# Second routed layer's front: fp32r subtraction on TensorE, two up parts moved there, gate weights ahead of the list's read-out

## The chip, the cores and the metric

The kernel runs on one core of one Trainium2 chip. The metric is the device time of one execution in microseconds (us), from the first to the last instruction of the core with what lies around it; lower is better.

## The reference, cut to what matters

Four layers act on 2048 rows of 256 floats, each added to its input: an attention, a mixture of 4 experts, an RWKV recurrence, and a mixture of 8 experts. The change lies at the start of the last one:

```python
x = hidden_states.reshape(-1, H)                       # 2048 rows of 256
logits = x @ gate_w.T + gate_b                         # 8 experts
top_vals, top_idx = jax.lax.top_k(logits, TOP_K)       # 2 of 8
routing = jax.nn.softmax(top_vals, axis=-1)
for e in range(E):
    h = x @ w1[e].T + b1[e]
    y = x_glu * jax.nn.sigmoid(1.702 * x_glu) * (x_lin + 1.0)
    out = out + (y @ w2[e].T + b2[e]) * we[:, None]
```

## The kernel before

A matrix product of float32 numbers is made from two fp32r parts of each factor: a high part (the number rounded to fp32r) and a low part (number minus high part, in fp32r). High by high, high by low and low by high are accumulated in PSUM. The weights of the experts therefore have to be split first. For the second mixture layer, `weight_units` cuts them into 12 parts of 128 x 1024: 8 up parts (w1 and w3, `k.up_parts`) and 4 down parts (w2). The original number lies in the low tile `f_w_lo`; ScalarE copies it into the high tile `f_w_hi` (`activation` Copy), and then it is replaced by the low part.

`second_front` does three things at once between the barrier after the RWKV phase and the first expert's product:

- **Ranking and lists.** VectorE (DVE) picks two experts for each token (`choose`, `pair`), counts (`place`), gives each choice a position (`positions`), and writes one-hot tables (`tables`: tile_oh, row_oh, tile_tok). TensorE (PE) multiplies tables (`Ranking.list`): 32 products of L941 give the token of every row of the tiles, and 16 products of L946 give the plane. VectorE then reads both out of PSUM (`rows`): `token_of`, and in three more operations `slot_of`. `weigh` makes the gate weights.
- **Splitting the up parts.** ScalarE `take_high`, then VectorE `take_low` (L879, a subtraction of two SBUF tiles), eight of each: two `take_low` before `rows`, six after, `weigh` at the end.
- **Splitting the down parts.** ScalarE `down_to_high` (L1322); TensorE `take_left` (for each half of 512 columns: identity times the number, L1302, then minus-identity times the high part, L1303, both as float32); ScalarE `down_to_low` (L1326) takes the difference out of PSUM. Two `take_left` stand ahead of `list` on TensorE, two behind it. `down_to_low` of one part must free the banks for a later `take_left`.

Each engine runs its instructions in the order written here; nothing is reordered but by hand. Part numbers n in `take_left(n)` and `down_to_low(n)` count from 0.

`expert_phase` follows in the same block with no barrier. GpSimd (POOL) waits for `rows_known` and then starts indirect gathers of token rows (L1423), one for each of the 39 tiles, 6 ahead. TensorE turns the rows of tiles 0 and 1 (L1469), ScalarE makes their high part (L1527), VectorE the low part (L1571), and `up(0)` (L1488) multiplies; it waits for all up parts. The first `turn_h` waits for all down parts. Then tiles follow in a fixed cycle, and the results are scattered with `slot_of` (L1437).

Of the kernel before, what the change touches and what calls it, by code (L numbers as in the profile page):

```python
# [884 lines left out]
class Ranking:  # L885

    def __init__(self, nc, m, v, k, ctx):
# [21 lines left out]
         self.zeros_ready, self.tiles_known, self.first_plane, self.numbered) = (  # L909
            sem(n) for n in "step exponentials_done picks ranked rows_ready counted named planed "  # L910
            "zeros_ready tiles_known first_plane numbered".split())
# [42 lines left out]
class RankSteps:  # L954
# [82 lines left out]
    def rows(self):  # L1037
        t, dve, then, k = self.t, self.dve, self.then, self.k
        dve.wait_ge(t.named, 1)
        then(dve.tensor_scalar(k.token_of[:], t.named_psum, float(TOK), None, ALU.add))  # L1040
        then(dve.scalar_tensor_tensor(out=t.unused[:], in0=t.named_psum, scalar=0.0, in1=t.neg_spare[:],
# [4 lines left out]
        then(dve.scalar_tensor_tensor(out=k.slot_of[:], in0=t.unused[:], scalar=2.0 * TOK, in1=t.named_psum,  # L1046
                                      op0=ALU.add, op1=ALU.add))
        k.rows_known = (t.step, self.done)
# [34 lines left out]
def first_front(nc, m, v, k, ctx, block):  # L1083
# [15 lines left out]
    parts, take_low = weight_units(v, k)  # L1099
    k.all_known = ((k.hi_done, k.all_parts), (k.lo_done, k.all_parts))  # L1100
# [109 lines left out]
    def _(dve):  # L1210
# [49 lines left out]
        steps.rows()  # L1260
# [7 lines left out]
def second_front(nc, m, v, k, ctx, block):  # L1268
# [8 lines left out]
    AT_ROWS, BEFORE_LIST = 2, 2  # L1277
    down_parts = parts[k.up_parts:]
    down_high, down_left, down_low, neg_zero, neg_ready = (
        sem(n) for n in "down_high down_left down_low neg_zero neg_ready".split())  # L1280
    k.all_known = ((down_high, len(down_parts)), (down_low, len(down_parts)))
    neg_ident = ctx.enter_context(nc.sbuf_tensor(f"{v.tag}r_neg_ident", [P, P], F32))
    flat = lambda part: f32(part).rearrange("p e n -> p (e n)")
    left = lambda n: (m.banks[:, 4:6, :] if n == 1 else m.banks[:, 6:8, :]).rearrange("p b n -> p (b n)")

    @block.gpsimd
    def _(pool):
        rank.clear(pool)
        pool.memset(neg_ident[:], 0.0).then_inc(neg_zero, 1)
        pool.wait_ge(neg_zero, 1)  # L1290
        pool.affine_select(out=neg_ident[:], in_=neg_ident[:], compare_op=ALU.not_equal, fill=-1.0, base=0,
                           pattern=[[-1, P]], channel_multiplier=1).then_inc(neg_ready, 1)

    @block.tensor
    def _(pe):
        def take_left(n):
            hi, lo = down_parts[n]
            pe.wait_ge(down_high, n + 1)
            at_least(pe, down_low, (0, 0, 1, 3)[n])
# [15 lines left out]
    def _(act):  # L1315
# [23 lines left out]
        for n in range(1, 5):  # L1339
            take_high(n)  # L1340
# [1041 lines left out]
```

## Time and profile before

| | |
|---|---|
| median of 3 runs | 732.92 us (732.75 to 733.7) |
| the profiled execution's own time | 731.65 us |
| its span, first to last instruction | 729.7 us |
| mean granted TensorE clock | 0.952 of full speed |
| busy share: PE, DVE, ACT, POOL | 90%, 71%, 48%, 46% |
| front of the second mixture layer, first DVE operation to first expert product | 566.33 to 597.18 us |
| its experts, first product to last scatter landed | 597.18 to 707.8 us |

The times of the table's last two rows are positions in the span. The profiled execution lies 1.95 us over its span, and 1.27 us under the median.

### The profile page before, as it was taken

The page shows a single profiled execution, that of the slowest core. Times are in us where ns is not written, and L with a number is a line of the kernel's source. Part 1 is how long each engine was busy: PE and PEld are TensorE (multiplying, and loading weights), DVE is VectorE, ACT ScalarE, POOL GpSimd, SP SyncE. Part 2 cuts the span into 40 slices and gives each one's busy share as a digit, 9 for nine tenths or more (in the row PEclk, how much of TensorE's full clock was granted, in tenths as well). Part 3 has the DMA queues.
Part 4 walks back from the last instruction along what each step waited for, and adds up shares of the span by engine and source line. Part 5 has one row for each costly group of instructions (what it writes and reads, how often), then busy time and mean ns, then how long its engine had stood idle before and what let it go on. Part 6 is the DMA issues. An engine that isn't in the chain of part 4 may idle for free. (4 is left out here: it accounts for less than half of the span.)

```text
span 729.7 us, 13761 instructions
## 1 busy us (share of the span) xinstructions
PE 660.3 (90%) x4339; PEld 538.6 (74%) x4339; DVE 518.9 (71%) x1087; ACT 349.0 (48%) x735; POOL 337.1 (46%) x326
## 2 busy tenths in 40 slices
PE   8989999879989999999997999999988679999950
PEld 6656666568868888888886888888877348888840
DVE  5878888957865555544444699998782868888847
ACT  1767777736403333333333565554552844554420
POOL 4977767510053344334224255555331066777530
PEclk9999999998999999999999999999976799999985
DMA  6900000101013111111106940000010022333229
GB/s 197 337 2 3 1 2 15 45 11 53 1 56 105 58 59 51 52 58 55 34 22 206 363 146 2 1 0 1 30 58 30 1 65 76 101 101 102 78 81 311
DMA packets 37185, 54.23 MB, mean 74 GB/s; under 512 B 6644, under 2 KB 28918, under 8 KB 36982
## 3 DMA queue, kind: packets, MB, share of 16 engines
q1 hardware_dynamic: 27832, 31.78, 13.0%
q0 software_dynamic: 7104, 19.41, 8.5%
q10 hardware_dynamic: 2176, 2.10, 0.9%
q8 instruction: 42, 0.69, 0.4%
q14 instruction: 31, 0.25, 0.1%
HBM read 37.28 MB, written 15.99 MB: 73 GB/s over the span
## 5 line engine op out<-in xcount | busy, mean ns | idle before, releaser
L1926 PE MATMUL banks<-r_xt,r_w_mixed 128*128 128x256 f32 x384 | 84.9, 380 | 0.7 <-ACT r_xt L2023 0.7
L1577 DVE SCALAR_TENSOR_TENSOR f0x_s<-f0x_th,banks 128x512 f32<-128x512 f32 x35 | 24.1, 687 | 83.2 <-ACT f0x_th L1536 83.2
L1437 POOL DMA_INDIRECT f_y<-f0x_yout,f_slot_of x35 | 34.5, 984 | 99.6 <-ACT f0x_yout L1552 99.6
L1926 PEld LDWEIGHTS banks<-r_xt,r_w_mixed 128*128 128x128 f32 x384 | 72.1, 189 | 11.0 <-ACT r_xt L2023 1.0
L1536 ACT ACTIVATE f0x_th<-banks 128x512 f32<-128x512 f32 x35 | 21.0, 600 | 86.9 <-PE banks L1488 86.9
L1423 POOL DMA_INDIRECT f0x_xg<-f_xn,f_token_of x35 | 34.9, 996 | 55.7 <-DVE f_slot_of L1046 44.3
L659 DVE TENSOR_REDUCE a_ssum<-a_e 128x6 f32<-128x1536 f32 x32 | 56.0, 1748 | 1.3 <-ACT a_e L526 1.0
L1488 PE MATMUL banks<-f_w_hi,f0x_xt_hi 128*128 x140 | 55.4, 396 | 0.9 <-DVE f0x_xt_lo L1571 0.9
L1488 PE MATMUL banks<-f_w_lo,f0x_xt_hi 128*128 x140 | 55.6, 397 | 0.0
L1423 POOL DMA_INDIRECT f1x_xg<-f_xn,f_token_of x39 | 40.6, 1041 | 32.4 <-DVE f_slot_of L1046 19.3
L1488 PE MATMUL banks<-f_w_hi,f0x_xt_lo 128*128 x140 | 55.2, 394 | 0.0
L526 ACT ACTIVATE a_e<-banks 128x1536 f32<-128x1536 f32 x32 | 46.6, 1455 | 13.9 <-PE banks L402 13.9
L1437 POOL DMA_INDIRECT f_y<-f1x_yout,f_slot_of x39 | 38.9, 997 | 27.4 <-ACT f1x_yout L1552 27.1
L757 POOL TENSOR_TENSOR a_rr<-a_ms_eps,neg_half 128x32 f32<-128x32 f32 (+1 forms) x9 | 44.0, 4888 | 15.3 <-DVE a_ms_eps L627 15.3
L1512 PE MATMUL banks<-f_w_hi,f0x_ht_hi 128*128 x140 | 42.4, 302 | 0.7 <-ACT f0x_yout L1552 0.7
L1512 PE MATMUL banks<-f_w_lo,f0x_ht_hi 128*128 x140 | 39.4, 281 | 0.0
L1512 PE MATMUL banks<-f_w_hi,f0x_ht_lo 128*128 x140 | 39.3, 281 | 0.0
L402 PE MATMUL banks<-a_ut,a_qt 32*128 32x256 f32 x512 | 36.7, 400 | 2.9 <-ACT a_e L516 2.1
L427 PE MATMUL banks<-a_e,a_vv 128*32 128x256 f32 x512 | 34.3, 385 | 1.7 <-DVE a_vv L674 1.5
L402 PEld LDWEIGHTS banks<-a_ut,a_qt 32*128 32x128 f32 x512 | 23.2, 184 | 16.9 <-ACT a_e L516 8.0
L1545 ACT ACTIVATE f1x_ht_hi<-banks 128x256 fp32r<-128x256 f32 x39 | 15.0, 385 | 40.5 <-PE banks L1499 40.5
L1589 DVE TENSOR_TENSOR f1x_hb<-banks,f_b 128x512 f32<-128x512 f32 x39 | 27.0, 691 | 9.3 <-PE banks L1488 9.3
(368 smaller groups left out, 1895.9 us busy)
## 6 DMA issues: line engine op xcount, KB each, us to landing
f_w_lo<-in_f_w13T SPq DMA_DIRECT2D x4, 2048.0 KB, 11.1
r_y<-f_y SPq DMA_DIRECT2D x16, 256.0 KB, 4.9
f_w_lo<-in_f_w2T SPq DMA_DIRECT2D x4, 512.0 KB, 15.1
f_xn<-f_rows_normed SPq DMA_DIRECT2D x8, 256.0 KB, 2.1
f_b<-in_f_b SPq DMA_DIRECT2D x1, 2048.0 KB, 10.1
f_w_lo<-in_f_w2T SPq DMA_DIRECT2D x2, 1024.0 KB, 11.9
f_xn<-r_y SPq DMA_DIRECT2D x8, 256.0 KB
f1c_y<-f_y SPq DMA_DIRECT2D x8, 256.0 KB, 7.8
```

The costliest lines, as they stand in the source:

```text
L402: last = pe.matmul(scores[:, i, s, :], qt[rows, b % 2, e, k, s * P:(s + 1) * P], ut[rows, b % 2, k, :], start=True, stop=True)
L427: last = pe.matmul(av(n)[32 * i:32 * i + 32, :], values[:, b % 2, head, :, :].rearrange("p r d -> p (r d)"), side[:, S * i + s, :], start= ...
L526: act.activation(ebuf[:, n % 3, 0:SUMS_ON_DVE, :], scores[:, 0:SUMS_ON_DVE // S].rearrange("p i s t -> p (i s) t"), ACT.Exp).then_inc(exp_ ...
L659: dve.tensor_reduce(ssum[:, b % 2, NB * p:NB * p + SUMS_ON_DVE], ebuf[:, n % 3, 0:SUMS_ON_DVE, :], AX_X, ALU.add).then_inc(sum_done, 1)
L757: pool.tensor_tensor(part(rr[:]), part(ms_eps[:]), part(m.neg_half[:, 0:S * NH]), ALU.pow).then_inc(rr_found, 1)
L1423: pool.indirect_dma_start(xg[:, t % GB, :], None, k.xn_dram, bass.IndirectOffsetOnAxis(ap=k.token_of[:, t:t + 1], axis=0)).then_inc(gather ...
L1437: pool.indirect_dma_start(k.y_dram, bass.IndirectOffsetOnAxis(ap=k.slot_of[:, done:done + 1], axis=0), yout[:, done % YB, :], None).then_i ...
L1488: last = pe.matmul(out, xt[a][:, t % 2, kb * P:(kb + 1) * P], k.weights[c][0][kb][:, e, cols], start=(i == 0), stop=(i == len(steps) - 1))
L1512: last = pe.matmul(y_psum(t), ht[a][:, t % 2, hb * P:(hb + 1) * P], k.weights[c][1][hb][:, e, :], start=(i == 0 and not v.lin_bias), stop= ...
L1577: dve.scalar_tensor_tensor(out=s1[:, t % 2, :], in0=th[:, t % 2, :], scalar=1.0, in1=glu_part, op0=ALU.add, op1=ALU.mult).then_inc(s1_done, 1)
L1589: dve.tensor_tensor(hb1[:, t % 2, :], up_banks(t), k.b1[:, e, :].rearrange("p e n -> p (e n)"), ALU.add).then_inc(hb1_done, 1)
L1926: last = pe.matmul(bank(1 + kind)[:, eb * T:(eb + 1) * T], r.w_mixed[:, kind, j // KB, j % KB, eb * P:(eb + 1) * P], xt[:, b % 2, j % KB, ...
```

## The change

Seven edits, the first six in `second_front` or in functions it calls. The subtracting product of `take_left` takes the high part and minus-identity as fp32r instead of float32. The last two up parts go the way of the down parts (`left_parts`, six of them; `PLAIN` is 6), so VectorE's `take_low` is called six times instead of eight. TensorE does four `take_left` ahead of `list` and two behind it, and waits for the fifth low part before it goes on. The PSUM banks for them alternate between two pairs. ScalarE's order is written anew. `weigh` moves from the end of VectorE's queue to just before the list's read-out, which is split into `tokens` (1 operation) and `slots` (3 operations); one `take_low` stands between them where two stood before both. GpSimd's gathers wait for the tokens and the tables' last reading by TensorE instead of for `slot_of`; only the first scatter waits for `slot_of` (in the first mixture layer the gathers wait for all three).

```diff
-    def rows(self):
+    def tokens(self):
         dve.wait_ge(t.named, 1)
         then(dve.tensor_scalar(k.token_of[:], t.named_psum, float(TOK), None, ALU.add))
+        k.tokens_known = (t.step, self.done)
+
+    def slots(self):
         then(dve.scalar_tensor_tensor(out=t.unused[:], in0=t.named_psum, scalar=0.0, in1=t.neg_spare[:],
                                       op0=ALU.is_equal, op1=ALU.mult))
         dve.wait_ge(t.planed, 1)
...
-        k.rows_known = (t.step, self.done)
+        dve.scalar_tensor_tensor(out=k.slot_of[:], ...).then_inc(t.slotted, 1)
@@ second_front
-    AT_ROWS, BEFORE_LIST = 2, 2
+    BY_PRODUCT = 2
+    down_parts, side_parts = parts[k.up_parts:], parts[k.up_parts - BY_PRODUCT:k.up_parts]
+    PLAIN = k.up_parts - BY_PRODUCT
+    left_parts = down_parts + side_parts
+    k.up_known = ((k.hi_done, PLAIN), (k.lo_done, PLAIN), (left_low, len(left_parts)))
+    k.all_known = ((left_high, len(left_parts)), (left_low, len(left_parts)))
+    neg_ident = ctx.enter_context(nc.sbuf_tensor(f"{v.tag}r_neg_ident", [P, P], F32R))
+    left = lambda n: m.banks[:, 4 + 2 * (n % 2):6 + 2 * (n % 2), :].rearrange("p b n -> p (b n)")
@@ TensorE
-            at_least(pe, down_low, (0, 0, 1, 3)[n])
+            at_least(pe, left_low, n - 1)
             for half in range(2):
-                pe.matmul(left(n)[:, cols], m.ident[:], flat(lo)[:, cols], start=True, stop=False)
+                pe.matmul(left(n)[:, cols], m.ident[:], f32(flat(lo))[:, cols], start=True, stop=False)
                 last = pe.matmul(left(n)[:, cols], neg_ident[:], flat(hi)[:, cols], start=False, stop=True)
-        for n in range(BEFORE_LIST):
+        for n in range(len(down_parts)):
             take_left(n)
         rank.list(pe)
-        for n in range(BEFORE_LIST, len(down_parts)):
+        for n in range(len(down_parts), len(left_parts)):
             take_left(n)
+        pe.wait_ge(left_low, len(left_parts) - 1)
@@ ScalarE, after the exponentials
-        down_to_high(2)
-        down_to_low(0)
-        down_to_high(3)
-        take_high(0)
-        down_to_low(1)
+        left_to_high(2)
+        left_to_high(3)
+        left_to_low(0)
+        left_to_high(4)
+        left_to_low(1)
         rank.negate(act)
-        for n in range(1, 5):
-            take_high(n)
-        down_to_low(2)
-        for n in range(5, k.up_parts):
-            take_high(n)
-        down_to_low(3)
+        left_to_low(2)
+        left_to_high(5)
+        left_to_low(3)
+        for n in range(PLAIN):
+            take_high(n)
+        left_to_low(4)
+        left_to_low(5)
@@ VectorE
         steps.experts()
-        for n in range(AT_ROWS):
-            take_low(dve, n)
-        steps.rows()
-        for n in range(AT_ROWS, k.up_parts):
-            take_low(dve, n)
-        steps.weigh()
+        steps.weigh()
+        steps.tokens()
+        take_low(dve, 0)
+        steps.slots()
+        for n in range(1, PLAIN):
+            take_low(dve, n)
@@ expert_phase, GpSimd
-        pool.wait_ge(*k.rows_known)
+        pool.wait_ge(*k.tokens_known)
+        pool.wait_ge(*k.tables_read)
+        if r:
+            pool.wait_ge(*k.slots_known)
...
+                if done == 0 and not r:
+                    pool.wait_ge(*k.slots_known)
@@ expert_phase, TensorE, before up(0)
-                    pe.wait_ge(k.hi_done, k.up_parts)
-                    pe.wait_ge(k.lo_done, k.up_parts)
+                    for semaphore, value in k.up_known:
+                        pe.wait_ge(semaphore, value)
```

`tables_read` is the semaphore `planed`, which the last L946 product raises.

## Rows read from the trace of the kernel before

**Rows 1.** The page: busy time of TensorE and the others, whole span.

```profile
PE 660.3 (90%) x4339; PEld 538.6 (74%) x4339; DVE 518.9 (71%) x1087; ACT 349.0 (48%) x735; POOL 337.1 (46%) x326
```

**Rows 2.** The chain that ended last, 570 to 600 us: start, length, what.

```profile
581.44 2.79 PE banks L941 x32
...
585.54 1.85 PE banks L1302 x2
...
590.23 1.03 ACT f_w_lo L1326
...
595.11 1.02 ACT f_w_lo L1326
...
597.18 1.67 PE banks L1488 x6
```

**Rows 3.** Windows: stretch, length, busy time by engine, granted clock, DMA share, GB/s.

```profile
570.88:574.07 3.19, 3.19 (x7) 2.03 (x8) 1.99 (x8) 3.19 (x4) 0.00 (x0) 0.50 0.00 0
574.07:580.01 5.94, 5.94 (x14) 2.28 (x12) 5.50 (x17) 3.31 (x4) 0.00 (x0) 1.00 0.00 0
...
581.44:585.54 4.10, 4.10 (x49) 4.10 (x50) 3.93 (x9) 4.10 (x5) 0.00 (x0) 0.85 0.02 4
585.54:590.23 4.69, 4.66 (x8) 1.71 (x8) 3.97 (x6) 0.00 (x1) 3.56 (x2) 0.77 0.10 28
```

**Rows 4.** Timeline of TensorE, `take_left`: start, length, line, names.

```profile
571.89 1.92 PE L1302 MATMUL banks<-f_w_lo,ident 128*128 128x512 f32 x2
...
573.60 1.26 PE L1303 MATMUL banks<-f_w_hi,f1r_neg_ident 128*128 128x512 f32 x2
...
593.19 1.02 PE L1302 MATMUL banks<-f_w_lo,ident 128*128 128x512 f32 x2
594.05 1.02 PE L1303 MATMUL banks<-f_w_hi,f1r_neg_ident 128*128 128x512 f32 x2
```

**Rows 5.** Timeline of VectorE: last table, experts, subtractions, weights; idle before in brackets.

```profile
580.59 0.80 DVE L1025 TENSOR_TENSOR f1k_tile_tok<-f1k_tile_oh,f1k_token 128x1248 f16<-128x1248 f16 x1
...
582.70 0.18 DVE L1034 CAST f_expert_of<-f1k_ef 128x39 int32<-128x39 f32 x1
582.92 2.36 DVE L879 TENSOR_TENSOR f_w_lo<-f_w_lo,f_w_hi 128x1024 fp32r<-128x1024 f32 x2
...
586.12 3.50 DVE L879 TENSOR_TENSOR f_w_lo<-f_w_lo,f_w_hi 128x1024 fp32r<-128x1024 f32 x3
592.23 3.50 DVE L879 TENSOR_TENSOR f_w_lo<-f_w_lo,f_w_hi 128x1024 fp32r<-128x1024 f32 x3 [2.62 <-ACT f_w_hi L1318]
595.65 0.17 DVE L1056 TENSOR_SCALAR f1k_total<-f1k_ex 128x16 f32<-128x16 f32 x1
```

**Rows 6.** Timeline of ScalarE: third high part, first low part, four up parts.

```profile
573.42 1.04 ACT L1322 ACTIVATE f_w_hi<-f_w_lo 128x1024 fp32r<-128x1024 f32 x1
576.62 1.02 ACT L1326 ACTIVATE f_w_lo<-banks 128x1024 fp32r<-128x1024 f32 x1 [2.15 <-PE banks L1303]
...
581.59 3.96 ACT L1318 ACTIVATE f_w_hi<-f_w_lo 128x1024 fp32r<-128x1024 f32 x4
```

**Rows 7.** Timeline of GpSimd: gathers 0, 1 and 3.

```profile
586.37 1.91 POOL L1423 DMA_INDIRECT f1x_xg<-f_xn,f_token_of  x1 [19.27 <-DVE f_slot_of L1046]
588.59 1.85 POOL L1423 DMA_INDIRECT f1x_xg<-f_xn,f_token_of  x1 [0.30 <-issue]
...
592.00 0.95 POOL L1423 DMA_INDIRECT f1x_xg<-f_xn,f_token_of  x1 [0.31 <-issue]
```

**Rows 8.** The tile of gathered rows, first mixture layer: from issue to landing.

```profile
DMA to landing us min/median/max: 2.7/2.8/4.7
```

**Rows 9.** The chain, in the experts' steady cycle: six fp32r products of 512 columns.

```profile
605.28 1.40 PE banks L1488 x6
```

**Rows 10.** Windows in the first mixture layer: pause before its list, list, stretch behind it.

```profile
200.21:202.38 2.17, 0.01 (x1) 0.00 (x1) 2.17 (x3) 0.60 (x1) 0.00 (x0) 1.00 0.00 0
...
206.19:209.40 3.21, 3.18 (x8) 2.23 (x8) 2.75 (x4) 0.00 (x0) 2.08 (x2) 0.59 0.00 0
```

More of the change, by code:

```diff
@@ L1040, in rows @@
         then(dve.tensor_scalar(k.token_of[:], t.named_psum, float(TOK), None, ALU.add))
+        k.tokens_known = (t.step, self.done)
+    def slots(self):
+        t, dve, then, k = self.t, self.dve, self.then, self.k
         then(dve.scalar_tensor_tensor(out=t.unused[:], in0=t.named_psum, scalar=0.0, in1=t.neg_spare[:],
@@ L1045, in rows @@
                                       op0=ALU.mult, op1=ALU.subtract))
-        then(dve.scalar_tensor_tensor(out=k.slot_of[:], in0=t.unused[:], scalar=2.0 * TOK, in1=t.named_psum,
-                                      op0=ALU.add, op1=ALU.add))
-        k.rows_known = (t.step, self.done)
+        dve.scalar_tensor_tensor(out=k.slot_of[:], in0=t.unused[:], scalar=2.0 * TOK, in1=t.named_psum,
+                                 op0=ALU.add, op1=ALU.add).then_inc(t.slotted, 1)
     def weigh(self):
@@ L1099, in first_front @@
     parts, take_low = weight_units(v, k)
+    k.up_known = ((k.hi_done, k.up_parts), (k.lo_done, k.up_parts))
     k.all_known = ((k.hi_done, k.all_parts), (k.lo_done, k.all_parts))
@@ L1276, in second_front @@
     parts, take_low = weight_units(v, k)
-    AT_ROWS, BEFORE_LIST = 2, 2
[L1278 to L1284, printed above, removed]
+    BY_PRODUCT = 2
+    down_parts, side_parts = parts[k.up_parts:], parts[k.up_parts - BY_PRODUCT:k.up_parts]
+    PLAIN = k.up_parts - BY_PRODUCT
+    left_parts = down_parts + side_parts
+    left_high, left_made, left_low, neg_zero, neg_ready = (
+        sem(n) for n in "left_high left_made left_low neg_zero neg_ready".split())
+    k.up_known = ((k.hi_done, PLAIN), (k.lo_done, PLAIN), (left_low, len(left_parts)))
+    k.all_known = ((left_high, len(left_parts)), (left_low, len(left_parts)))
+    neg_ident = ctx.enter_context(nc.sbuf_tensor(f"{v.tag}r_neg_ident", [P, P], F32R))
+    flat = lambda part: part.rearrange("p e n -> p (e n)")
+    left = lambda n: m.banks[:, 4 + 2 * (n % 2):6 + 2 * (n % 2), :].rearrange("p b n -> p (b n)")
     @block.gpsimd
@@ L1358, in _ @@
         steps.experts()
-        for n in range(AT_ROWS):
+        steps.weigh()
+        steps.tokens()
+        take_low(dve, 0)
+        steps.slots()
+        for n in range(1, PLAIN):
             take_low(dve, n)
-        steps.rows()
-        for n in range(AT_ROWS, k.up_parts):
-            take_low(dve, n)
-        steps.weigh()
 def expert_phase(nc, m, v, k, ctx, block, A, r):
```

31 lines of the change are left out of this document (16 added, 15 removed).

## The prediction, made before the changed kernel was run

> **What bounds the kernel now.** I read the page first. TensorE is busy 90% of the span [rows 1], so what it waits for is what can be won. Next the chain that ended last, around the place of the change. Up to the tables the front of the second mixture layer is a chain of small VectorE operations, which the change leaves alone; it ends when L1025 ends at 581.39 [rows 5]. From there the chain runs on TensorE: list and planes 581.44 to 585.54, then the two `take_left` behind the list, with the low parts that ScalarE takes at 590.23 and 595.11, and then the first expert product at 597.18 [rows 2]. What the reader is to see: from 585.54 to 595.11 the experts wait for TensorE to subtract two down parts. VectorE's own subtractions end at 592.23 + 3.50 = 595.73 [rows 5], so they are late by nearly as much; a change that relieved only one of the two would gain little. Then the windows, for the clock: it stood at 0.50 (1.2 GHz) until 574.07, at 1.00 (2.4 GHz) until the list, and was 0.85 and 0.77 in the mean in the list and the stretch behind it [rows 3]. Last the timelines of the four other engines, for who is next.
>
> Behind 597.18 the experts run in TensorE's cycle, and everything after hangs on it. I take a shift of the first product to reach the end one for one.
>
> **The subtracting pass.** At full clock L1302 starts at 593.19 and L1303 at 594.05: a float32 product of 512 columns costs 0.86 us, and a `take_left` has four, 3.44 us [rows 4]. At half clock it is 573.60 - 571.89 = 1.71 [rows 4]. An fp32r product of 512 columns costs 1.40/6 = 0.23 [rows 9]. The new pass has that shape and type, with another stationary tile, so I take 0.23 (0.43 to 0.46 at half clock). From above its cost is bounded by today's 0.86; from below I exclude under 0.21, since 1.40/6 is already nearly 512 columns at 2.4 GHz. A `take_left` becomes 2 x (0.86 + 0.23) = 2.18.
>
> **TensorE ahead of the list, four `take_left` instead of two.** The first: starts at 571.89, L1302 at half clock to 573.60, the pass 0.45 to 574.05; the clock rises at 574.07 as before, since up to 573.60 TensorE does the same; 0.86 + 0.23 end it at 575.14. Three more at 2.18 end at 581.68. Do they wait? `take_left(2)` needs the low part 0, `take_left(3)` the low part 1. ScalarE takes high parts 2 and 3 from 573.42, each about 1.0 [rows 6], until 575.4, low 0 until 576.5, high 4 until 577.5, then low 1 (TensorE's second is done at 577.5 with the drain) until 578.6. TensorE wants them at 577.3 and 579.5. So no wait, with 0.9 to spare. The list begins at 581.68 instead of 581.44: **+0.24**. List and planes take 4.10 [rows 3] and end at 585.78.
>
> **Behind the list, again two `take_left`.** Before: from 585.54 to ScalarE's start at 595.11, 9.57 us, in which TensorE also waited about 1.2 for ScalarE's low part of 590.23 [rows 2]. That wait goes: the banks of part 4 were emptied with low 2 (about 581), those of part 5 with low 3 (about 583). After, with the clock down as long as now: L1302 about 1.85 [rows 2], pass 0.43, then 0.86 and 0.23, second part 2.18, drain 0.15: 5.70 us, to 591.48. **-3.87.** From ScalarE's start on the last low part to the first product it took 597.18 - 595.11 = 2.07 [rows 2], and the same steps stand there: low part, high part of x, low part of x. The first product starts at 593.55.
>
> **Does ScalarE get there?** Its low 2 is at 580.8, high 5 at 581.8, low 3 (TensorE's fourth ends at 581.85) at 582.9. Six `take_high` at 3.96/4 = 0.98 [rows 6] end at 588.9, low 4 at 589.9. It waits for TensorE at 591.5, so it is not the bound. It has two low parts more than before, 2 x 1.02 [rows 6], where it used to wait.
>
> **VectorE.** `experts` ends at 582.88. `weigh` costs 0.66 (595.65 to about 596.31, three operations that begin with the row shown) [rows 5], to 583.6; it lies in the time in which the list is still being made. If that cover were gone it would cost its 0.66, which it costs today behind the last subtraction. The token list is ready at about 584.6 (list's end 584.23 [rows 2] plus 0.24 and a hand-over of 0.1) and read in 0.2. A subtraction costs 3.50 for three, 1.14 from start to start and 1.22 the last [rows 5]. One goes to 585.95, `slots` is 0.7 (of the 0.92 that the four reading operations have between 585.20 and 586.12, and planes are there by 585.9), to 586.65, and five more to 586.65 + 4 x 1.14 + 1.22 = 592.43. Their high parts are there at 588.9. So two subtractions less (-2.3), no wait for ScalarE (2.62 before [rows 5]), and about 1.6 later since only one comes before the slots and none before the tokens. VectorE alone would let the first product start at 592.43 + 0.05 + 0.43 for x's low part + 0.19 = 593.1. It is the next in line, 0.45 behind TensorE.
>
> **GpSimd.** Gathers now need the tokens (584.8) and the planes' last product (585.78), so the first starts at about 586.1 instead of 586.37. Gathers 0 and 1 took 1.91 and 1.85, gather 3 took 0.95 though a subtraction began during it [rows 7]. Gather 0 began inside a subtraction of 586.12 and ended 0.94 after that one's end: a gather that starts during L879 is held till it ends, one already running is not. In the new order gather 0 falls into `slots` (587.1), gather 1 starts at 587.4 in the subtraction that ends at 587.87, is out at 588.8, and lands 2.7 less 0.95 later [rows 8], at 590.6. `turn_x(0)` comes at 591.3. Hidden, by 0.7. The first scatter's wait for `slot_of` (586.65) costs nothing; a scatter needs the first result, 8 us after the first product.
>
> **First mixture layer.** GpSimd waits for two more semaphores, VectorE for one less; bounds -0.1 and +0.2 (two hand-overs), taken as 0.
>
> **Sum.** +0.24 - 3.87 = -3.63, first product at 593.55. The profiled execution took 731.65, so 728.0. The median of the three runs is 1.27 above it: 732.92 - 3.6 = **729.3 us**. Of a gain under 0.2% (1.5 us) I would not say that a measurement tells it from none.
>
> **The rivals.**
>
> *The clock doesn't fall (729.3 becomes 728.8), chance 0.15.* Before the list TensorE paused from 580.01 to 581.44, then the clock fell in the middle of the list. The new order has no pause there. Also in the first mixture layer a pause of 2.17 stands before the list, and the stretch behind it has 0.59 [rows 10]. Then the two last `take_left` cost 4.36 + 0.15, end at 590.3, and VectorE binds: 593.1, or -4.1. Against it: the list's products themselves are small, TensorE is busy in all 4.10 us of them [rows 3], and the fall comes there. The Trainium skill (TensorE: Matmul & The Clock Gate, What's actually happening) has the clock lowered after idleness; by it alone this rival would be the likelier. The fall in a busy list is why I don't follow it.
>
> *The clock falls later or longer, chance 0.13.* If it falls at the list's end and stays down the 3.4 us that it does now (584.3 to 587.7), it is at half until 589.2: low part 5 starts at 592.0 and the first product at 594.1, -3.1, 729.8. If it stays down through both `take_left`, they cost 2 x 2 x (1.71 + 0.43) = 8.6, the first product comes at 596.6, -0.6, 732.3. I give the latter 0.04.
>
> *Gathers bind, 0.07.* If GpSimd loses every turn against the back-to-back subtractions and its second gather only gets out after 592.4, it lands at 595.1 and the first product comes at about 596.5: -0.7, 732.2. Against it gather 1, which got out during three subtractions in a row.
>
> *Slower: the pass isn't cheap, 0.05.* If it costs what L1303 costs now, 0.86, the four parts end at 576.41 + 3 x 3.44 = 586.7, the list is 5.3 late and VectorE stands behind it in its wait for the tokens. TensorE's last two parts end at 586.7 + 4.1 + 8.3 = 599.1, the first product comes at 601.1: +3.9, 736.8. Twelve passes lie on the path, so it decides from 0.23 + 3.63/12 = 0.53 a pass on, and is slower by 0.2% from 0.66. Nothing in the rows shows this price for fp32r.
>
> *The change does little at the end, 0.05.* The front is shorter, but the experts' cycle starts with new waits (gathers, two fewer buffers ahead) and takes 2 us back. The steady cycle shows TensorE full, so I see no place for it.
>
> **Numbers.** Forecast 0.55 with its own range 728.8 to 729.9, the full clock 0.15, later or longer clock 0.13 (0.04 of it at 732.3), gathers 0.07, slower 0.05, little 0.05. Range 728.4 to 731.2: from the full clock less 0.4 for two runs of one kernel differing, to half of what the gathers and the long slow clock could cost. Faster: 0.55 + 0.15 + 0.09 + a part of the gathers and of the little, 0.86. Same: 0.09. Slower: 0.05.
>
> **What the new profile would show.** L1303 with 8 records near 0.4 us long, one for each product, 0.23 from start to start with its neighbour. The list at 581.7. ScalarE's low 1 before 579.5. No idle of VectorE in front of a subtraction. The granted clock in the stretch behind the list: 0.77 as before, or 1.00 (rival). The first L1488 at 593.5, with the wait before it by x's low part, and the last low part of ScalarE at 591.5. The prediction is wrong if TensorE idles between the four first `take_left`, if the list starts after 582.5, or if L1469 waits for a gather.

## The result and the profile after

The changed kernel takes 728.53 us (median of 6 runs, 727.83 to 729.23), the kernel before 732.84 in the same comparison: ratio 0.9942, 95% interval 0.993 to 0.9955, that is 4.3 us less (3.3 to 5.1). Forecast were 729.3 us and a gain of 3.6. A later comparison gave 0.9956 (0.9941 to 0.9971), that is 3.2 us by the ratio and 2.5 us by the medians. One of the six executions of an experiment below (gathers wait for slot_of) took 855.42 us with a mean granted clock of 0.734; its row and ratio leave it out. The profiled execution took 727.92 us with a span of 726.2; its TensorE clock was 0.952 in the mean, as before.

Line numbers have moved: L1302 and L1303 are L1311 and L1312, L1326 is L1336, L1423 is L1434, L941 is L942, L1469 is L1485, L1488 is L1504, L1571 is L1587; the experiments shift them by a few lines more. Positions are also shifted: the front's first VectorE operation starts at 565.91 here and at 566.33 in the profile of before, though nothing ahead of it but the first layer's read-out was changed. I therefore measure the front by two lengths that begin there:

- **L**, to the first expert product: 597.18 - 566.33 = 30.85 before, 593.92 - 565.91 = 28.01 after.
- **M**, to the start of the last scatter: 705.34 - 566.33 = 139.01 before, 702.11 - 565.91 = 136.20 after. It holds the experts too, and so a clock that is down at their start.

The timeline of the changed kernel, for these lengths and for what each engine did last:

```profile
565.91 0.29 DVE L1359 TENSOR_TENSOR f_logits<-banks,f_gate_b 128x128 f32<-128x128 f32 x1 [7.43 <-PEq L2312]
...
580.17 0.80 DVE L1026 TENSOR_TENSOR f1k_tile_tok<-f1k_tile_oh,f1k_token 128x1248 f16<-128x1248 f16 x1
...
581.93 2.78 PE L942 MATMUL banks<-f1k_tile_tok,f1k_row_oh 128*128 128x39 f16 x32
...
585.06 1.23 DVE L879 TENSOR_TENSOR f_w_lo<-f_w_lo,f_w_hi 128x1024 fp32r<-128x1024 f32 x1
...
586.77 5.76 DVE L879 TENSOR_TENSOR f_w_lo<-f_w_lo,f_w_hi 128x1024 fp32r<-128x1024 f32 x5
586.83 2.10 POOL L1434 DMA_INDIRECT f1x_xg<-f_xn,f_token_of  x1 [20.15 <-DVE f1k_unused L1049]
...
589.24 1.85 POOL L1434 DMA_INDIRECT f1x_xg<-f_xn,f_token_of  x1 [0.30 <-issue]
...
591.84 1.02 ACT L1336 ACTIVATE f_w_lo<-banks 128x1024 fp32r<-128x1024 f32 x1 [1.15 <-PE banks L1312]
...
592.95 0.44 PE L1485 MATMUL banks<-ident,f1x_xg 128*128 128x128 f32 x2 [0.93 <-DMA f1x_xg<-f_xn,f_token_of]
593.17 0.42 DVE L1587 TENSOR_TENSOR f1x_xt_lo<-banks,f1x_xt_hi 128x256 fp32r<-128x256 f32 x1 [0.64 <-ACT f1x_xt_hi L1543]
...
593.92 0.49 PE L1504 MATMUL banks<-f_w_hi,f1x_xt_hi 128*128 x1 [0.53 <-ACT f1x_xt_hi L1543]
...
702.11 0.97 POOL L1453 DMA_INDIRECT f_y<-f1x_yout,f_slot_of  x1 [0.34 <-ACT f1x_yout L1568]
```

Three things end within a microsecond: ScalarE's last low part at 592.86, VectorE's last subtraction at 586.77 + 5.76 = 592.53, the second gather's landing at 592.91. Before, ScalarE's was at 596.13, VectorE's at 595.73, and GpSimd had started the second gather's transfer by 590.44, 6.7 us before the first product [rows 2, 5, 7].

The chain that ended last, same kernel:

```profile
573.40 0.43 PE banks L1312
573.83 1.50 PE banks L1311 x2
575.33 0.23 PE banks L1312
...
581.86 0.23 PE banks L1312
582.09 2.64 PE banks L942 x32
...
586.83 2.10 POOL f1x_xg L1434
...
589.24 3.67 DMA f1x_xg<-f_xn,f_token_of
...
592.95 0.45 PE banks L1485 x2
...
593.92 1.67 PE banks L1504 x6
```

The reader is to see three things. The pass costs 0.23 at full clock and 0.43 at half. The list follows straight on the fourth part, where before it waited for the tables; TensorE, not the tables, now starts it. And behind the list the chain no longer runs through TensorE's products but through a gather; that is a close race, not a long wait.

The granted clock, by windows of the same kernel:

```profile
571.49:574.95 3.46, 3.46 (x7) 1.68 (x6) 2.85 (x11) 3.46 (x5) 0.00 (x0) 0.50 0.00 0
575.05:581.80 6.75, 6.75 (x20) 3.41 (x18) 6.47 (x15) 5.46 (x6) 0.00 (x0) 1.00 0.00 0
582.00:585.20 3.20, 3.20 (x42) 3.20 (x42) 1.33 (x8) 3.07 (x4) 0.00 (x0) 1.00 0.02 5
585.30:588.60 3.30, 3.30 (x13) 2.01 (x12) 3.23 (x6) 3.30 (x4) 1.77 (x1) 0.50 0.00 0
588.60:592.00 3.40, 3.40 (x11) 1.61 (x9) 3.40 (x4) 1.47 (x3) 2.79 (x3) 0.99 0.18 51
```

The clock rose at 575.0, 9.1 us after the front's start; before it was 574.07 - 566.33 = 7.7 [rows 3]. It fell at 585.2, 3.3 us into the list, and rose at 588.6; in the kernel before it fell at 584.3, 2.9 us into the list, and rose at 587.7. So it is down for 3.4 us in both.

### The profile page after: what moved, and what is told of

The parts are those of the page before. It is cut to its first block and busy times, and to the rows that moved or that the text cites. A ratio compares the mean times of both kernels' runs of the same rounds, so it can differ in the third digit from the quotient of the medians.

```text
span 726.2 us, 13774 instructions
## 1 busy us (share of the span) xinstructions
PE 658.5 (91%) x4343; PEld 537.6 (74%) x4343; DVE 516.5 (71%) x1085; ACT 351.2 (48%) x737; POOL 336.4 (46%) x326
## 5 line engine op out<-in xcount | busy, mean ns | idle before, releaser
L1434 POOL DMA_INDIRECT f0x_xg<-f_xn,f_token_of x35 | 34.1, 973 | 56.3 <-DVE f_slot_of L1051 44.8
L1504 PE MATMUL banks<-f_w_hi,f0x_xt_hi 128*128 x140 | 55.4, 396 | 0.9 <-DVE f0x_xt_lo L1587 0.9
L1504 PE MATMUL banks<-f_w_lo,f0x_xt_hi 128*128 x140 | 55.6, 397 | 0.0
L1434 POOL DMA_INDIRECT f1x_xg<-f_xn,f_token_of x39 | 40.7, 1043 | 31.7 <-DVE f1k_unused L1049 20.2
L1504 PE MATMUL banks<-f_w_hi,f0x_xt_lo 128*128 x140 | 55.2, 394 | 0.0
L526 ACT ACTIVATE a_e<-banks 128x1536 f32<-128x1536 f32 x32 | 46.6, 1456 | 15.1 <-PE banks L402 15.1
```

The source lines that it names most:

```text
L526: act.activation(ebuf[:, n % 3, 0:SUMS_ON_DVE, :], scores[:, 0:SUMS_ON_DVE // S].rearrange("p i s t -> p (i s) t"), ACT.Exp).then_inc(exp_ ...
L1434: pool.indirect_dma_start(xg[:, t % GB, :], None, k.xn_dram, bass.IndirectOffsetOnAxis(ap=k.token_of[:, t:t + 1], axis=0)).then_inc(gather ...
L1504: last = pe.matmul(out, xt[a][:, t % 2, kb * P:(kb + 1) * P], k.weights[c][0][kb][:, e, cols], start=(i == 0), stop=(i == len(steps) - 1))
```

## The experiments

Times are against the kernel before in the same set of runs. The set of the changed kernel is the one above. Three sets followed, with medians of the kernel before of 732.31, 732.73 and 732.22 us: first the pass in float32, the pass alone, no up part, and gathers that wait for slot_of; then the filled pause, weights last, early products and combined; then the split read-out, the changed kernel again, the early products again, and the weights behind slot_of. L and M come from one profiled execution of each. A ratio can differ a little from that of the medians.

| run | time, us | ratio to before (95%) | L | M |
|---|---|---|---|---|
| before (profile shown ahead) | 732.84 | | 30.85 | 139.01 |
| changed | 728.53 | 0.9942 (0.993 to 0.9955) | 28.01 | 136.20 |
| changed, again | 729.68 | 0.9956 (0.9941 to 0.9971) | 27.68 | 136.19 |
| pass in float32 | 735.29 | 1.004 (1.0027 to 1.0053) | 34.05 | 142.16 |
| before, fp32r pass alone | 732.50 | 1.0005 (0.9991 to 1.0018) | 30.87 | 139.04 |
| the same, pause filled | 732.11 | 0.9996 (0.9982 to 1.001) | 30.10 | 139.85 |
| before, split read-out alone | 732.28 | 1.0006 (0.9994 to 1.0018) | 31.41 | 139.83 |
| changed, no up part on TensorE | 730.75 | 0.9984 (0.9971 to 0.9996) | 29.42 | 138.87 |
| changed, gathers wait for slot_of | 728.31 | 0.9948 (0.9933 to 0.9963) | 27.87 | 135.95 |
| changed, weights last | 728.93 | 0.9951 (0.9933 to 0.9969) | 28.14 | 136.26 |
| changed, early products | 726.98 | 0.9925 (0.9907 to 0.9943) | 27.32 | 135.67 |
| the same again | 727.69 | 0.9946 (0.9932 to 0.9961) | 27.27 | 135.49 |
| combined | 728.50 | 0.9938 (0.9919 to 0.9957) | 27.55 | 135.79 |
| combined, weights behind slot_of | 727.14 | 0.9933 (0.992 to 0.9947) | 26.56 | 134.80 |

**The pass in float32 again.** Everything else as changed.

```diff
-    neg_ident = ctx.enter_context(nc.sbuf_tensor(f"{v.tag}r_neg_ident", [P, P], F32R))
+    neg_ident = ctx.enter_context(nc.sbuf_tensor(f"{v.tag}r_neg_ident", [P, P], F32))
...
-                last = pe.matmul(left(n)[:, cols], neg_ident[:], flat(hi)[:, cols], start=False, stop=True)
+                last = pe.matmul(left(n)[:, cols], neg_ident[:], f32(flat(hi))[:, cols], start=False, stop=True)
```

> The changed kernel with one part undone: minus-identity and the high part go into the subtracting product as float32 again. I measure the front by L, from VectorE's first operation in it (the logits) to the first expert product; L was 30.85 us before and 28.01 after the change. Theory (the order of TensorE's work only pays since the pass is cheap): the four parts ahead of the list take 4.5 + 3 x 3.44 = 14.8 us, the list starts 5.3 later than before, the two parts behind it cost 8.3: L about 34.9, the kernel about 4 us slower than before, near 737. Rival (VectorE's two subtractions less are the gain, the pass does not matter): L at most 29.5, the kernel still faster than before.

Measured: L 34.05, 3.0 us slower. The list's first row in its timeline, and the read-out behind it:

```profile
588.26 2.81 PE L942 MATMUL banks<-f1k_tile_tok,f1k_row_oh 128*128 128x39 f16 x32
...
591.18 0.20 DVE L1041 TENSOR_SCALAR f_token_of<-banks 128x39 uint32<-128x39 f32 x1 [6.70 <-PE banks L942]
```

With the front's start at 567.24 the list starts 21.0 us into it, 5.9 later than before (581.44 - 566.33 = 15.1), and VectorE stands 6.70 us in its wait. The rival falls: the new order pays only with the cheap pass, and without it the change makes the kernel slower. L is 0.8 under what I expected, since the clock never fell: it was 1.00 from 576.2 on, through the list and both parts behind it.

**The fp32r pass alone, in the kernel before**, with its orders and eight subtractions.

```diff
-    neg_ident = ctx.enter_context(nc.sbuf_tensor(f"{v.tag}r_neg_ident", [P, P], F32))
-    flat = lambda part: f32(part).rearrange("p e n -> p (e n)")
+    neg_ident = ctx.enter_context(nc.sbuf_tensor(f"{v.tag}r_neg_ident", [P, P], F32R))
+    flat = lambda part: part.rearrange("p e n -> p (e n)")
...
-                pe.matmul(left(n)[:, cols], m.ident[:], flat(lo)[:, cols], start=True, stop=False)
+                pe.matmul(left(n)[:, cols], m.ident[:], f32(flat(lo))[:, cols], start=True, stop=False)
```

> The kernel before with one part alone: the subtracting product in fp32r. All orders and the eight VectorE subtractions stay. Theory (two engines are late side by side): TensorE's part behind the list ends at 589.1 instead of 590.2, ScalarE's three last high parts follow it, VectorE ends its subtractions and the weights at about 595.2, and the first product comes at 595.9: L about 29.6, gain 1.3 us, near 731.5. Rival (the pass is the whole gain): L near 28.0, the time of the changed kernel, 728.5.

Measured: L 30.87, no gain. Both theories fall. Its windows:

```profile
574.90:578.50 3.60, 3.56 (x10) 1.56 (x9) 3.19 (x15) 2.76 (x4) 0.00 (x0) 0.99 0.00 0
578.50:582.46 3.96, 0.00 (x0) 0.00 (x1) 3.93 (x6) 3.96 (x5) 0.00 (x0) 0.92 0.00 0
582.46:586.60 4.14, 4.14 (x49) 4.14 (x50) 3.97 (x9) 2.13 (x3) 0.00 (x0) 0.50 0.01 4
586.60:590.90 4.30, 4.30 (x6) 1.59 (x6) 3.92 (x6) 0.00 (x0) 3.20 (x2) 0.50 0.10 30
590.90:595.20 4.30, 3.10 (x5) 1.51 (x5) 2.17 (x2) 3.86 (x4) 3.39 (x4) 0.50 0.32 91
```

The two parts ahead of the list end sooner, TensorE pauses 4.0 us instead of 1.43, the clock falls at 581.8, before the list has begun, and stays at 0.50 until 595.5, though TensorE was busy in all 8.44 us from 582.46 to 590.90. What the pass saves, the slower float32 products beside it cost. I formed a third theory, that the gain was lost to the clock, and tried it.

**The pause filled.**

```diff
         for n in range(BEFORE_LIST):
             take_left(n)
+        for n in range(16):
+            pe.matmul(m.banks[:, 2, 0:P], m.ident[:], m.ones[:], start=True, stop=True)
         rank.list(pe)
```

> The kernel before with the fp32r pass alone, and 16 products of the identity with the tile of ones (128 columns, float32, into a bank that the list overwrites) put into TensorE's pause between the second part and the list; they add nothing to the output. With the pass alone TensorE paused 4.0 us there, its clock stood at 0.50 from 581.9 to 595.3, and L (VectorE's first operation of the front to the first expert product) was 30.87, as before the change. Theory (the cheaper pass's time was lost to the clock): the clock falls later or for about 3.4 us only, as in the kernel before, L is 29.6 within 0.4, the kernel 1.0 to 1.5 us faster than the pass alone. Rival (VectorE and ScalarE eat the gain, the clock is incidental): L stays at 30.9.

Measured: L 30.10, 0.77 shorter than with the pass alone, the theory's direction but about 0.6 of its size; the clock was down from 585.7 to 589.1 only, as long as in the kernel before. What limits L is now VectorE:

```profile
591.87 3.50 DVE L879 TENSOR_TENSOR f_w_lo<-f_w_lo,f_w_hi 128x1024 fp32r<-128x1024 f32 x3 [1.87 <-ACT f_w_hi L1320]
...
593.63 1.01 ACT L1328 ACTIVATE f_w_lo<-banks 128x1024 fp32r<-128x1024 f32 x1
```

ScalarE's last low part starts 26.9 us into the front, against 28.8 in the kernel before. VectorE's last of eight subtractions ends at 28.7, against 29.4. TensorE's side came 1.9 us earlier, and the first product only 0.75. M is 139.85, longer than before: TensorE, done early, waited 2.92 us for the low part of x, the clock fell again at 596.0 and was down until 602.8, in the first experts. The time is that of the kernel before (0.9996). So the clock took the pass's gain in the run with the pass alone, and in this one VectorE took a part of it and the clock in the first experts the rest. The windows and rows show where the time lies; that filling brings the gain back is not shown.

**No up part on TensorE.** VectorE subtracts eight.

```diff
-    BY_PRODUCT = 2
+    BY_PRODUCT = 0
@@ ScalarE
-        left_to_high(4)
...
-        left_to_high(5)
...
-        left_to_low(4)
-        left_to_low(5)
```

> The changed kernel with one part undone: no up part goes through TensorE, VectorE subtracts all eight; the four down parts stay ahead of the list. Theory (VectorE is the next in line): its subtractions end 2 x 1.14 = 2.3 us later than the 592.5 of the changed kernel, the first product comes at about 595.5: L about 29.6, 1.5 us slower than the changed kernel, near 730.1. Rival (TensorE's parts behind the list or the gathers bind, the subtractions are hidden): L near 28.0 or under it, 728.5.

Measured: L 29.42, 1.41 longer than the changed kernel's 28.01: the theory, to 0.2. M is 138.87, 2.67 longer, and here is the reason:

```profile
586.20:595.57 9.37, 1.39 (x6) 0.59 (x5) 9.30 (x13) 5.53 (x8) 7.61 (x4) 0.50 0.14 42
595.57:599.00 3.43, 3.43 (x9) 2.74 (x10) 0.48 (x2) 0.00 (x0) 2.52 (x4) 0.50 0.25 76
```

TensorE, with nothing behind the list, is busy 1.39 of 9.37 us; the clock, down since 585.4, stays at 0.50 until 599.0, and the first experts run at half speed. So the two up parts do two things: they take 2 x 1.14 us from VectorE, and they keep TensorE at work until the experts begin. The first is worth about 1.4 us of L, and what comes on top in M, 1.3 us, is the clock. In time it is 730.75 against 728.31 for the kernel whose gathers wait for slot_of, of the same set, 2.4 us. That the clock is what comes on top is read from these windows; no run keeps the clock up there without the two parts.

**Gathers wait for slot_of alone.**

```diff
-        pool.wait_ge(*k.tokens_known)
-        pool.wait_ge(*k.tables_read)
-        if r:
-            pool.wait_ge(*k.slots_known)
+        pool.wait_ge(*k.slots_known)
...
-                if done == 0 and not r:
-                    pool.wait_ge(*k.slots_known)
```

> The changed kernel with one part undone: in both mixture layers the gathers wait for slot_of alone, one wait instead of two or three. In the changed kernel's trace the first gather of the second mixture layer began at 586.83, 0.8 us after the last planes product, and that of the first one 0.98 us after slot_of, where it was 0.30 in the kernel before. Theory (the gathers are held by VectorE's subtractions, not by the semaphores): the first gather of the second layer still ends about 0.94 after the same subtraction, L stays at 28.0 within 0.2, the time is that of the changed kernel. Rival (the split read-out lets the gathers begin earlier and that is worth something): L grows by 0.5 or more. A third point is whether the separate waits themselves cost GpSimd time: then the first layer's gather comes back to 0.3 after slot_of.

Measured: L 27.87, the time of the changed kernel. The theory holds. In this run's timeline:

```profile
206.85 0.19 DVE L1051 SCALAR_TENSOR_TENSOR f_slot_of<-f0k_unused,banks 128x35 uint32<-128x35 f32 x1
...
207.34 1.93 POOL L1434 DMA_INDIRECT f0x_xg<-f_xn,f_token_of  x1 [44.41 <-DVE f_slot_of L1051]
...
586.79 1.79 POOL L1434 DMA_INDIRECT f1x_xg<-f_xn,f_token_of  x1 [20.43 <-DVE f_slot_of L1051]
```

Letting the gathers go before slot_of gains next to nothing: the first one of the second layer starts 586.79 - 565.58 = 21.2 us into the front here, 20.9 in the changed kernel. The third point came out too: the first layer's gather is back to 0.30 after slot_of, from 0.98.

**The weights last.**

```diff
-        steps.weigh()
         steps.tokens()
         take_low(dve, 0)
         steps.slots()
         for n in range(1, PLAIN):
             take_low(dve, n)
+        steps.weigh()
```

> The changed kernel with one part undone: the gate weights are made behind the last subtraction again. Theory (their 0.66 us lie in VectorE's wait for the list, and VectorE has slack to the last low part): the first low part of x would start at 593.2 instead of 593.17, L stays within 0.2 of 28.0. Rival (the move is a part of the gain): L grows by 0.5 to 0.7, the time by as much.

Measured: L 28.14, M 136.26. The rival falls: L is 0.13 longer, which is less than two profiles of the changed kernel differ by (0.33), so that move is worth nothing that shows here.

**The split read-out alone, in the kernel before.** The edits of `tokens`, `slots` and `expert_phase`'s GpSimd from the diff ahead, both layers:

```diff
-        steps.rows()
+        steps.tokens()
+        steps.slots()
...
-        pool.wait_ge(*k.rows_known)
+        pool.wait_ge(*k.tokens_known)
+        pool.wait_ge(*k.tables_read)
+        if r:
+            pool.wait_ge(*k.slots_known)
```

> The kernel before with one part alone, in both mixture layers: the read-out split into tokens and slots, and the gathers waiting for tokens and the tables' last reading (in the first layer for slot_of too). Subtractions, TensorE and ScalarE are those of before. I measure the stretch M from VectorE's first operation of the second front to the start of the last scatter, which takes in a clock that is down in the first experts: 139.0 us before, 136.2 after the change. Theory (all of the gain lies in the second front's products and subtractions): L and M as before, 30.9 and 139.0 within 0.2, no difference in time. Rival (part of the measured 4.3 us, of which the profiled front showed only 2.8, comes from the split read-out in the first layer): about 1 us faster than before with L and M unchanged. The first gather of each layer should again start 0.8 to 1.0 after its last semaphore, where one wait has 0.3.

Measured: no difference in time (1.0006), so no gain of a size that these intervals show comes from the first layer. But the theory misses L and M: L is 31.41 and M 139.83, not 30.85 and 139.01. The clock rose 9.0 us after the front's start here, not 7.7, and it fell at 19.3, not 18.0. TensorE does the same in both kernels until then. The later rise costs nothing ahead of the list, since the list waits for the tables and starts 15.11 us into the front in both. The later fall costs: more of the 3.4 us at half clock lies on float32 products of 512 columns. The chain of this run:

```profile
585.12 1.65 PE banks L1307 x2
586.77 1.71 PE banks L1308 x2
...
595.20 1.02 ACT f_w_lo L1331
```

L1308 is L1303 of before, where these two products took 1.09 (587.39 to 588.48). The last low part starts 29.33 us into the front, 0.55 later than before, which is all of L's 0.56. So the profile of the kernel before caught a short front, and with the clock's rise and fall at the same place (9.0 and 19.3; 9.1 and 19.3) the change is worth 31.41 - 28.01 = 3.40 in L and 3.63 in M.

**The changed kernel again.**

> The changed kernel once more, beside the others of this call. If its front is steady L is 28.0 and M 136.2 within 0.2. The time from the kernel's start to the second front's first operation differed by up to 2.6 us among the profiles so far, both ways; theory: that is what one execution differs from another, and the changed kernel is near 4 us faster than before with 2.8 to 3.6 of it in M. Rival: M is another by more than 0.5, so one profile does not tell the front's gain.

Measured: L 27.68, M 136.19, 3.2 us faster than before by the ratio, 2.5 by the medians. M repeats to 0.01, L to 0.33: here the clock rose at 8.1, and it fell once more for 3.4 us at the start of the experts, which gives it back. The theory holds for M, with L 0.1 outside of its bound. The start of the front lay at 567.99, 2.1 us from the first profile: that is what executions differ by.

**Early products.**

```diff
+        for n in range(10):
+            pe.matmul(m.banks[:, 2, 0:P], m.ident[:], m.ones[:], start=True, stop=True)
         rank.count(pe)
         pe.wait_ge(neg_ready, 1)
```

> The changed kernel with 10 products of the identity with the tile of ones (128 columns, float32, into a bank that the list overwrites) on TensorE at the front's start, before the counting products; they add nothing to the output. In the changed kernel the clock rose at 575.0, 9.1 us after the front's start, where I had forecast 574.07 - 566.33 = 7.7, and TensorE, not the tables, started the list: 0.9 late. Theory (the forecast's missing 0.8 us of the front are the clock's later rise): the clock is up when the first part begins or soon after, the four parts end before the tables are ready, the list starts as soon as they are, L is 27.1 within 0.3, about 0.9 us faster than the changed kernel, near 727.6. Rival (gathers or VectorE bind the first product anyway): L stays at 28.0.

Measured: L 27.32, M 135.67, 726.98 us. Windows of this run, and two rows of its timeline:

```profile
565.00:570.50 5.50, 5.50 (x24) 5.24 (x25) 4.39 (x15) 5.49 (x5) 0.61 (x3) 0.50 0.00 0
570.60:580.10 9.50, 9.12 (x26) 4.28 (x25) 8.71 (x25) 9.17 (x12) 0.00 (x0) 1.00 0.01 2
```

```profile
570.57 1.02 PE L1311 MATMUL banks<-f_w_lo,ident 128*128 128x512 f32 x2
...
580.07 2.86 PE L942 MATMUL banks<-f1k_tile_tok,f1k_row_oh 128*128 128x39 f16 x32 [0.35 <-DVE f1k_tile_tok L1026]
```

The clock is up when the first part begins, the row of its two records is 1.02 us long there instead of 1.92, and the list waits for the tables again. It starts 580.07 - 565.00 = 15.07 us into the front, 0.95 sooner than in the changed kernel, and L gets 0.69 of that. That is near the 0.79 by which the forecast missed L.

> The changed kernel with the 10 early products once more, beside the changed kernel itself. L was 27.3 and M 135.7, against 28.0 and 136.2. Theory: the front is 0.5 to 0.7 us shorter by the clock's earlier rise, and the time by as much; the 1.5 us between the medians of two calls were chance for the rest. Rival: the gain in time is the whole 1.5 us.

Measured: L 27.27, M 135.49, 727.69 us, beside 729.68 for the changed kernel. The front's gain repeats (0.4 to 0.7 in L and M). The medians differ by 2.0 us here, the ratios of the same two kernels by 0.7 us (0.9946 and 0.9956), and the intervals overlap. The 1.5 us of the first time compares medians of two sets. So I give the gain as 0.4 to 0.7 us by the front; that the time gains more is not shown.

**Combined.** The early products, and:

```diff
@@ TensorE: halves of the fifth part on either side of the list
+        take_left(4, (0,))
         rank.list(pe)
-        for n in range(len(down_parts), len(left_parts)):
-            take_left(n)
+        take_left(4, (1,))
+        take_left(5)
@@ ScalarE: the first up part's copy earlier
-        left_to_high(5)
+        take_high(0)
         left_to_low(3)
-        for n in range(PLAIN):
+        left_to_high(5)
+        for n in range(1, PLAIN):
@@ VectorE
         steps.weigh()
+        take_low(dve, 0)
         steps.tokens()
-        take_low(dve, 0)
+        take_low(dve, 1)
         steps.slots()
-        for n in range(1, PLAIN):
+        for n in range(2, PLAIN):
```

> A version that may beat the changed kernel: the 10 early products; half of the fifth part ahead of the list, in the time the faster clock frees; the first up part's high copy moved forward on ScalarE, so that VectorE subtracts one part while it waits for the list and one more between the read-outs. Theory (three engines are late within half a microsecond of one another, so all three must be relieved): TensorE's last part ends at about 24.3 us after the front's start (25.8 in the changed kernel), VectorE's subtractions at 25.3 (26.6), the gathers are out earlier by as much as the list, L is 26.6 within 0.4, 1.4 us faster than the changed kernel. Rival (the early products alone do it): L as in the run with them alone.

Measured: L 27.55, a miss, no better than the early products alone. Three engines were earlier (ScalarE's last low part began 24.6 us into the front, against 25.9), and the gathers were not:

```profile
588.09 4.62 DVE L879 TENSOR_TENSOR f_w_lo<-f_w_lo,f_w_hi 128x1024 fp32r<-128x1024 f32 x4
...
588.22 2.03 POOL L1441 DMA_INDIRECT f1x_xg<-f_xn,f_token_of  x1 [19.81 <-DVE f1k_unused L1049]
...
594.22 0.44 PE L1492 MATMUL banks<-ident,f1x_xg 128*128 128x128 f32 x2 [1.66 <-DMA f1x_xg<-f_xn,f_token_of]
```

The first gather began 0.13 us after a subtraction. The last low part starts 24.62 us into the front, 0.7 earlier than with the early products alone, and the first product comes 2.93 us behind it instead of 1.96: TensorE waits 1.66 us for the second gather.

**The weights behind slot_of.** 0.66 us of small operations now stand where the subtraction did.

```diff
-        steps.weigh()
         take_low(dve, 0)
         steps.tokens()
         take_low(dve, 1)
         steps.slots()
+        steps.weigh()
```

> The combined version with the gate weights' three small operations moved behind slot_of. In the combined version TensorE, ScalarE and VectorE were all earlier, but the first gather began 0.13 us after a subtraction, was held to its end, took 2.03 us, the second was held again, landed at 594.2 and was what the first product waited for (L 27.55). Theory (a gather that starts in a subtraction is held to its end): now it starts beside the small operations, takes 0.95, the second one is out 1.1 us earlier; the first product waits for the low parts; L is 26.8 within 0.3, M 135.0. Rival (the gathers are slow for another reason, their waits or the DMA): L stays at 27.5 or grows by 0.66, the weights' time.

Measured: L 26.56, M 134.80, 727.14 us.

```profile
587.10 1.06 POOL L1441 DMA_INDIRECT f1x_xg<-f_xn,f_token_of  x1 [19.81 <-DVE f1k_unused L1049]
...
587.67 4.63 DVE L879 TENSOR_TENSOR f_w_lo<-f_w_lo,f_w_hi 128x1024 fp32r<-128x1024 f32 x4
588.47 1.25 POOL L1441 DMA_INDIRECT f1x_xg<-f_xn,f_token_of  x1 [0.30 <-issue]
...
593.08 0.49 PE L1511 MATMUL banks<-f_w_hi,f1x_xt_hi 128*128 x1 [1.08 <-DVE f1x_xt_lo L1594]
```

The first gather takes 1.06 instead of 2.03 and the first product waits for the low part of x again. L is 1.0 shorter than without the move, though VectorE's last subtraction ends 0.7 later (25.8 against 25.1 us into the front). The last low part starts at the same place (24.60 against 24.62), so the gathers are the whole 1.0: the first product comes 1.96 behind it again. The theory holds, and this is the shortest front: 1.4 us under the changed kernel in M. In time it is 2.5 us less in the medians of one set and 1.7 by the ratios, with intervals (0.992 to 0.9947, and 0.9941 to 0.9971) that overlap a little.

## Why the prediction was right, step by step

Steps in us from the front's start; those forecast are the prediction's positions less 566.33.

| step | forecast | changed kernel |
|---|---|---|
| clock up | 7.7 | 9.1 |
| list starts | 15.35 | 16.02 |
| last low part starts on ScalarE | 25.15 | 25.93 |
| VectorE's last subtraction ends | 26.1 | 26.6 |
| second gather landed | 24.3 | 27.0 |
| first product | 27.22 | 28.01 |

The 0.79 us between the last two figures are 0.67 ahead of the list, 0.11 behind it and 0.01 in the hand-over.

- **The pass** costs 0.23, as taken from [rows 9]; a half of a part is 1.09 (576.48 to 577.57 in the timeline). Right, and what the forecast hangs on. (The trace has one record of 0.80 for each of the twelve passes, not eight of 0.4; the cost is the step from start to start.) The float32 run puts the price of being wrong at 3.2 us of L over before, where the rival had 3.9.
- **Ahead of the list.** No waits between the four parts: right. That "the clock rises at 574.07 as before, since up to 573.60 TensorE does the same" was the step that was mis-sized. TensorE did the same, and the clock rose 1.35 us later by the front's start. At half speed that is 0.67 us, which is the list's whole lateness (16.02 - 15.35). It has nothing to do with the change: the kernel with the split read-out alone has the same TensorE work as before and its clock rose at 9.0. Among the fronts without early products the rise lay at 7.7, 7.7, 8.1 and seven times between 8.8 and 9.1.
- **Behind the list.** Forecast 5.70 from the list's end; 591.84 less 581.93 + 4.10 is 5.81. The clock fell and came back as now, the rival of a clock that does not fall was wrong. The hand-over of 2.07 was 593.92 - 591.84 = 2.08, in part by luck: it took another way (see the gathers).
- **VectorE next in line**: right. Two subtractions put back cost 1.41 of L. What I had not priced was that the two parts also keep TensorE busy behind the list; another 1.3 in M comes with that.
- **Gathers hidden by 0.7**: wrong, and "if L1469 waits for a gather" was one of the forecast's own signs of being wrong: L1485, the same line, waits 0.93 us for the second one. The first began at 20.9, not 19.8: 0.67 of that is the late list, and it came 0.8 us behind the last product of the planes where I had put 0.3. So it began in a subtraction (586.83 in one from 586.77) instead of in `slots`, and the second landed 2.7 later than forecast, 1.3 us after `turn_x(0)` began. In the sum it cost about 0.1, an estimate: the low part of x ends at 593.59, and the first product followed it by 0.2 where nothing else was late (596.99 to 597.18 in the kernel before); here it came at 593.92, right behind the work on the second gather's rows. But it was one more thing that ended within a microsecond, and it took the combined version's whole gain.
- **Weights, first layer** at nothing: right, by a run each.
- **Not tried alone**: the four parts ahead of the list with the pass cheap, the banks, ScalarE's order, and the one subtraction between the read-outs. What they bring can't be told apart; together with the cheap pass, the earlier weights and the split read-out they give the step from 30.85 or 31.41 to 29.42 (no up part on TensorE).
- **The sum.** Forecast -3.63. The profiles shown give -2.84 in L and -2.81 in M. Against the run in which the clock rose and fell where it did after the change it is -3.40 and -3.63. The timed gains are 4.3 and 3.2. So the mechanism and the size hold within what single executions differ by; which part of the 4.3 beyond 3.6 is more than chance is not settled.

The Trainium skill (TensorE: Matmul & The Clock Gate, What's actually happening) has the clock lowered after idleness. The traces bear that out on one side: with a 4.0 us pause the clock fell in front of the list and stayed down (pass alone), with TensorE nearly idle it stayed down for 13.6 us (no up part), and with no pause at all ahead of the list it did not fall in the float32 run. They do not on the other: in the changed kernel TensorE was busy without a pause from 571.49 to 592, and the clock fell at 585.2 all the same, in the list's small products. And with the pass alone it stayed down while TensorE was busy for 8.44 us on end.

## What to carry to other kernels

When two or three engines end within a microsecond, relieving one is worth little: with the pause filled TensorE's side came 1.9 us earlier and the first product 0.75, and the combined version only paid once the gathers were freed too. Work that ends early on TensorE can cost its gain in clock, so give it what other engines are late with, rather than a pause. And look at where a GpSimd gather starts among VectorE's two-input subtractions: 0.66 us of small operations put in at that place took 1.0 us off the front.

## What the runs showed of the hardware that I had not expected

- **The clock's rise varies.** For the same TensorE work it came 7.7 to 9.1 us after the front's start, and its fall moved with it (18.0 and 19.3 in the kernel before and with the split read-out alone), worth about 0.6 us in one profile. One profile is no measure of a gain of that size.
- **Waits on GpSimd aren't free.** With one semaphore awaited besides the rows' storing, the first layer's gather began 0.30 us after slot_of (before, and gathers waiting for slot_of alone). With three it began 0.97 or 0.98 after it, in all ten profiles of such kernels. In the changed kernel:

```profile
207.56 0.19 DVE L1051 SCALAR_TENSOR_TENSOR f_slot_of<-f0k_unused,banks 128x35 uint32<-128x35 f32 x1
...
208.73 1.26 POOL L1434 DMA_INDIRECT f0x_xg<-f_xn,f_token_of  x1 [44.83 <-DVE f_slot_of L1051]
```

  What in the waits costs the 0.7 us was not tried.
- **A gather that starts inside a subtraction is held to its end.** 2.03 against 1.06 us for a start 0.13 us after a subtraction's and one 0.57 before it. The Trainium skill (SBUF — State Buffer, SBUF: two separate sides) says that a VectorE instruction with two SBUF inputs and a GpSimd one that reads SBUF share a pair of ports, and that whichever starts first has it for its whole instruction. The trace agrees on the gather's side, with these numbers. It does not on the other: in the changed kernel five subtractions take 5.76 us, 1.14 from start to start and 1.22 the last, as in the kernel before [rows 5], though the first gather ran until 588.93, beside the second of them.
- **The clock falls in the list or at its end**, busy as TensorE is there, in every profile but two: the float32 one, where it never fell, and the pass alone, where it fell ahead of the list. It is down for 3.4 us where TensorE works on behind it. What tells the float32 run from the changed kernel, neither of which pauses ahead of the list, stays open.
